# Two DRAM tables for the sums of the first mixture, and its last two tiles added by TensorE through token marks

## The reference

```python
x = x + jnp.tanh(g_xattn[0]) * _L0_xattn_ref(_layernorm(x), ctx_512, ...)
x = x + jnp.tanh(g_ffn[0]) * _L0_ffn_ref(_layernorm(x), ...)        # first mixture
x = x + jnp.tanh(g_xattn[1]) * _L1_xattn_ref(ctx_512, _layernorm(x), ...)
x = x + jnp.tanh(g_ffn[1]) * _L1_ffn_ref(_layernorm(x), ...)        # second mixture
```

## Time and profile before

| what | value |
| --- | --- |
| median of 3 runs | 369.81 us (369.34 to 369.99) |
| time of the profiled execution | 369.4 us |
| its span, first to last instruction | 367.4 us |
| TensorE busy | 322.0 us, 88% of the span |
| VectorE, ScalarE, GpSimd busy | 205.4, 153.1, 109.4 us |
| mean granted clock of TensorE | 0.896 |
| share of the chain that ended last | PE 76%, DVE 11%, ACT 4%, issue 4%, DMA 2% |

### The profile page before, as it was taken

One profiled execution on the slowest core, in us unless ns is written; L12 is line 12 of the kernel. 1 busy time (PEld: TensorE's weight loads), 2 busy tenths in 40 slices (PEclk: granted clock), 3 DMA queues, 4 the chain that ended last, 5 costly groups with the idle time before them and its releaser, 6 DMA issues.

```text
span 367.4 us, 6937 instructions
## 1 busy us (share of the span) xinstructions
PE 322.0 (88%) x2144; PEld 185.0 (50%) x2144; DVE 205.4 (56%) x640; ACT 153.1 (42%) x339; POOL 109.4 (30%) x106
## 2 busy tenths in 40 slices
PE   8974599899999999999999999158878999989992
PEld 6643493555555555555555555047334444444440
DVE  1678874655554445555555542495936645455237
ACT  1565402133444343343344444267433545445541
POOL 0021131221333332222212221133234666563310
PEclk9995556999999999999999999655869999999995
DMA  7999919996927372554211112411222222331146
GB/s 236 346 309 319 299 40 287 282 271 199 239 38 245 81 214 41 164 122 133 31 37 14 16 14 29 93 38 59 72 58 55 75 88 87 83 77 58 45 145 228
DMA packets 21146, 48.40 MB, mean 132 GB/s; under 512 B 2600, under 2 KB 11688, under 8 KB 20088
## 3 DMA queue, kind: packets, MB, share of 16 engines
q1 hardware_dynamic: 14680, 35.78, 31.0%
q0 software_dynamic: 6048, 11.28, 14.4%
q10 hardware_dynamic: 384, 0.90, 0.8%
HBM read 37.98 MB, written 9.96 MB: 131 GB/s over the span
## 4 chain that ended last, share of the span: by engine, by line
PE 76%; DVE 11%; ACT 4%; issue 4%; DMA 2%; POOL 1%; ACTq 1%; another core or an unknown queue 1%; DVEq 0%; POOLq 0%
PE bank L1432 27%; PE bank L1406 23%; PE bank L1482 8%; PE bank L1396 6%; PE bank L1245 3%; PE bank L1253 3%; PE bank L1305 2%; DVE st L749 1%; DVE z L939 1%; DMA sums<-y_sb,route_dst 1%; DVE z L827 1%; PE bank L1374 1%; DMA rows<-sums 1%; PE bank L1325 1%; POOL fs L403 1%
## 5 line engine op out<-in xcount | busy, mean ns | idle before, releaser
L1432 PE MATMUL bank<-wgu,xT 128*64 x320 | 99.5, 465 | 1.5 <-issue 0.9
L1432 PE MATMUL bank<-rows,xT 128*64 128x344 f32 x320 | 99.5, 465 | 0.0
L1406 PE MATMUL bank<-wdn,hT 120*64 (+2 forms) x396 | 89.9, 392 | 8.5 <-ACT hT L583 6.8
L1406 PEld LDWEIGHTS bank<-wdn,hT 120*64 120x64 f32 (+1 forms) x396 | 48.9, 140 | 48.4 <-issue 23.0
L1432 PEld LDWEIGHTS bank<-wgu,xT 128*64 128x64 f32 x320 | 43.1, 140 | 47.5 <-issue 8.2
L423 POOL DMA_INDIRECT sums<-y_sb,route_dst x20 | 31.6, 1581 | 115.5 <-ACT y_sb L621 97.5
L415 POOL DMA_INDIRECT x_in<-rows,route_tok x43 | 42.7, 993 | 46.3 <-DVE route_tok L945 17.6
L1019 DVE SCALAR_TENSOR_TENSOR hh<-th,bank 128x344 f32<-128x344 f32 x40 | 20.5, 513 | 58.2 <-ACT th L571 58.2
L1406 PE MATMUL bank<-rows,hT 120*64 120x256 f32 x228 | 52.4, 379 | 0.0
L1432 PEld LDWEIGHTS bank<-rows,xT 128*64 128x64 f32 x320 | 43.1, 140 | 0.0
L571 ACT ACTIVATE th<-bank 128x344 f32<-128x344 f32 x40 | 18.3, 458 | 59.3 <-PE bank L1432 59.3
(11 more groups left out here) (172 smaller groups left out, 451.6 us busy)
## 6 DMA issues: line engine op xcount, KB each, us to landing
wgu<-gu SPq DMA_DIRECT2D x8, 1376.0 KB, 22.4
wdn<-wd SPq DMA_DIRECT2D x8, 720.0 KB, 27.0
wgu<-gu SPq DMA_DIRECT2D x3, 1408.0 KB, 7.1
wdn<-wd SPq DMA_DIRECT2D x5, 576.0 KB, 8.3
rows<-rows SPq DMA_DIRECT2D x8, 256.0 KB, 3.7
wgu<-results SPq DMA_DIRECT2D x4, 512.0 KB, 5.0
wgu<-gu SPq DMA_DIRECT2D x1, 1056.0 KB, 6.8
rows<-xt SPq DMA_DIRECT2D x4, 256.0 KB, 7.4
```

The lines of the kernel that those rows point to most:

```text
L1406: last = mm(psum[7][part, 0:H], hT[0:m.wide, j * P:(j + 1) * P][:, part], wd(j), start=(j == 0), stop=(j == m.chunks - 1))
L1432: last = mm(psum[2 * c + g][part, 0:CH0], xT[:, r, k * P:(k + 1) * P][:, part], w, start=(k == 0), stop=(k == KH - 1))
```

## The change

1. `sums` has 2 * (T + P) rows. Slots 64 to 127 of a tile add to the second table: const_f has one more column, C_HALF, with T + P in rows 64 and up, and `targets` adds it to the target row. The second table is filled with zeros by one more DMA behind the five base stores, from a block of y_sb that VectorE sets to zero first. `base_stored` then counts one more.
2. Only tiles 0 to 17 are scattered (ADDED = S0 - 2). The read-back waits for 18 scatters and for all gate and up matmuls, and reads both tables: the first to xs, the second to xn, eight DMAs, from the fourth on also behind the down matmuls of tile 18.
3. Tiles 18 and 19 stay in y_sb. In steps 2 and 3 VectorE makes marks from their tokens (`mark_tokens`): for each of the 8 blocks a 128x128 matrix is_here, with a one where the slot's token is that row. Behind the last down matmuls TensorE multiplies y_sb by the marks into four PSUM banks (`first_rest` for tile 18, `add_rest` for tile 19, of which 64 slots are in use). For batches 2 and 3 TensorE also adds the rows of the second table (xn through the identity). For batches 0 and 1 VectorE adds the two tables (`two_sums`).
4. `second(b)` first adds the two PSUM blocks of the batch to xs, and then does its statistics.
5. `edge` is no longer scaled and shifted ahead of time (L1146 goes). The shift goes into nmx with one more small instruction in `mix_terms`, the scale into `add_edge`, which becomes a scalar_tensor_tensor.
6. `edges(1)` on TensorE moves behind `add_rest(0)`, and on VectorE the shifts of its half (`edge_shifts(1)`) move behind mix_terms(0). The order of `mix_terms` and `add_edge` is changed.
7. The six semaphores for the second mixture's weights become one; who waits and where stays the same.

```diff
-    sums = nc.dram_tensor("sums", (T + P, H), fp32).ap()
+    sums = nc.dram_tensor("sums", (2 * (T + P), H), fp32).ap()
...
+            sp.wait_ge(zero_made, 1)
+            sp.dma_start(sums_t[:, NT + 1:2 * NT + 2, :],
+                         y_sb[:, 0:1, :].to_broadcast([P, NT + 1, H])).then_inc(base_stored, 16)
...
-                    sp.wait_ge(y_added, 16 * S0)
+                    sp.wait_ge(y_added, 16 * ADDED)
+                    sp.wait_ge(m.gu_done, 2 * S0)
                     for b in range(B):
                         sp.dma_start(xs[:, 2 * b:2 * b + 2, :], sums_t[:, 2 * b:2 * b + 2, :]).then_inc(m.y_here[b], 16)
+                        if b == 1:
+                            sp.wait_ge(m.y_done, S0 - 1)
+                        sp.dma_start(xn[:, 2 * b:2 * b + 2, :],
+                                     sums_t[:, NT + 1 + 2 * b:NT + 3 + 2 * b, :]).then_inc(m.y_here[b], 16)
...
-                    pool.wait_ge(m.y_copied, s + 1)
-                    scatter(m, s)
+                    if m.n == 1 or s < ADDED:
+                        pool.wait_ge(m.y_copied, s + 1)
+                        scatter(m, s)
...
+            def mark_tokens(q):
+
+                tile = ADDED + q
+                then(nc.vector.scalar_tensor_tensor(
+                    out=block_of[:], in0=cf[:, C_SLOT:C_SLOT + NT], scalar=-float(P),
+                    in1=m.tok[:, tile:tile + 1].to_broadcast([P, NT]), op0=ALU.mult, op1=ALU.add))
+                nc.vector.tensor_tensor(
+                    is_here[:, q], ch[:, H_LO:H_LO + P].unsqueeze(1).to_broadcast([P, NT, P]),
+                    block_of[:].unsqueeze(2).to_broadcast([P, NT, P]), ALU.is_equal).then_inc(marked, 1)
...
+            def two_sums(b):
+
+                dve.wait_ge(mix[0].y_here[b], 32)
+                for i in (2 * b, 2 * b + 1):
+                    last = did(nc.vector.tensor_tensor(xs[:, i, :], xn[:, i, :], xs[:, i, :], ALU.add))
+                return last
+
             def second(b):
-                dve.wait_ge(mix[0].y_here[b], 16)
+
+                if b >= 2:
+                    dve.wait_ge(mix[0].y_here[b], 32)
+                dve.wait_ge(rest_done, b + 1)
+                rest = m1.late_rows[b]
+                for i in (2 * b, 2 * b + 1):
+                    last = did(nc.vector.tensor_tensor(xs[:, i, :], rest[:, i % 2, :], xs[:, i, :], ALU.add))
+                after(last)
                 stats(rows_of_x, b, LN_EPS, 1.0, x2_var)
...
-                nc.vector.scalar_tensor_tensor(out=nmx[:, two], in0=mv[:, two, 0], scalar=-1.0, in1=cc[:, two],
-                                               op0=ALU.mult, op1=ALU.mult).then_inc(mix_ready, 1)
+                then(nc.vector.tensor_tensor(nmx[:, two], mv[:, two, 0], cc[:, two], ALU.mult))
+                nc.vector.scalar_tensor_tensor(out=nmx[:, two], in0=nmx[:, two], scalar=-1.0, in1=edge_shift[:, two],
+                                               op0=ALU.mult, op1=ALU.add).then_inc(mix_ready, 1)
...
+            edge_shifts(0)
+            added = (two_sums(0), two_sums(1))
+            after(added[0])
             second(0)
+            after(added[1])
             second(1)
             mix_terms(0)
-            for b in range(B):
-                if b + 2 < B:
-                    second(b + 2)
-                if b + 1 < B:
-                    mix_terms(b + 1)
-                add_edge(b)
+            edge_shifts(1)
+            second(2)
+            add_edge(0)
+            mix_terms(1)
+            second(3)
+            add_edge(1)
+            mix_terms(2)
+            mix_terms(3)
+            add_edge(2)
+            add_edge(3)
...
+            pe.wait_ge(marked, 2)
+            pe.wait_ge(mix[0].y_copied, S0 - 1)
+            for b in range(B):
+                first_rest(2 * b)
+            add_rest(0)
+            edges(1)
+            for b in range(1, B):
+                add_rest(b)
             pe.wait_ge(edge_th, NT)
             turn_x4(0)
```

More of the change, by code:

```diff
@@ L39 @@
 ONE_LAST = most_halves(E0) < 2 * S0
+ADDED = S0 - 2
 LATE = S1 + NT - NS
@@ L187, in build @@
         w0_order, first_staged, ends_ready = sem("w0_order"), sem("first_staged"), sem("ends_ready")
-        w1_here = [sem(f"w1_here{i}") for i, _ in enumerate(second_weights())]
+        w1_here = sem("w1_here")
+        W1_ALL = 16 * sum((gu_z > gu_a) + (dn_z > dn_a) for _, gu_a, gu_z, dn_a, dn_z in second_weights())
         out_stored = sem("out_stored")
@@ L248, in __init__ @@
                             for bank in ((2, 7, 0, 1) if n == 0 else (4, 5, 3, 6))]
+                if n == 1:
+                    m.late_rows = [psum[bank][:, :].rearrange("p (j h) -> p j h", j=2) for bank in (4, 5, 3, 6)]
                 m.ranks = psum[0 if n == 0 else 2][:, 0:(NT + 1) * experts].rearrange("p (i e) -> p i e", e=experts)
@@ L694, in stage_down1 @@
                                      ACT.Copy).then_inc(m1.dn_staged, 1)
-            for n, (_, gu_a, gu_z, dn_a, dn_z) in enumerate(second_weights()):
-                act.wait_ge(w1_here[n], 16 * (gu_z > gu_a) + 16 * (dn_z > dn_a))
+            act.wait_ge(w1_here, W1_ALL)
             for i in range(NS):
@@ L960, in targets @@
                                                  ALU.is_equal, ALU.mult))
-                    nc.vector.tensor_tensor(m.dst, m.tok, m.pad, ALU.add).then_inc(m.targets_ready, 1)
+                    nc.vector.scalar_tensor_tensor(out=m.dst, in0=m.tok, scalar=cf[:, C_HALF:C_HALF + 1], in1=m.pad,
+                                                   op0=ALU.add, op1=ALU.add).then_inc(m.targets_ready, 1)
                 else:
@@ L1138, in half_var, with edge_shifts @@
                                         ALU.mult, ALU.add).then_inc(m1.var, 1)
-            dve.wait_ge(edge_c_ready, 1)
-            for h in range(2):
+            def edge_shifts(h):
                 four = slice(4 * h, 4 * h + 4)
@@ L1193, in _ @@
             dve.wait_ge(m1.experts_ready, 1)
-            for n, (_, gu_a, gu_z, dn_a, dn_z) in enumerate(second_weights()):
-                dve.wait_ge(w1_here[n], 16 * (gu_z > gu_a) + 16 * (dn_z > dn_a))
+            dve.wait_ge(w1_here, W1_ALL)
             hidden_early(2)
@@ L1498, in gate_up_slots, with add_rest, first_rest @@
                          lambda k: stage_gu1[:, t % 2, k * 2 * F1:(k + 1) * 2 * F1])
-            pe.wait_ge(mix[0].y_copied, S0)
+            def add_rest(b):
+                pe.wait_ge(mix[0].y_copied, S0)
+                rest = m1.late_rows[b]
+                if b >= 2:
+                    pe.wait_ge(mix[0].y_here[b], 32)
+                for j in range(2):
+                    i = 2 * b + j
+                    if j == 1:
+                        first_rest(i)
+                    if b >= 2:
+                        mm(rest[:, j, :], ident, xn[:, i, :], start=False, stop=False)
+                    last = mm(rest[:, j, :], is_here[0:HALF, 1, i, :], y_sb[0:HALF, (S0 - 1) % RING, :],
+                              start=False, stop=True)
+                last.then_inc(rest_done, 1)
+            def first_rest(i):
+                mm(m1.late_rows[i // 2][:, i % 2, :], is_here[:, 0, i, :], y_sb[:, (S0 - 2) % RING, :],
+                   start=True, stop=False)
+            pe.wait_ge(marked, 2)
[6 more added lines that the diff above has]
+                add_rest(b)
             pe.wait_ge(edge_th, NT)
@@ L1507, in _ @@
             ranks(m1)
-            for n, (_, gu_a, gu_z, dn_a, dn_z) in enumerate(second_weights()):
-                pe.wait_ge(w1_here[n], 16 * (gu_z > gu_a) + 16 * (dn_z > dn_a))
+            pe.wait_ge(w1_here, W1_ALL)
             for i in range(NS):
```

41 lines of the change are left out of this document (24 added, 17 removed).

## The result

| what | before | after |
| --- | --- | --- |
| median, same chip, 7 runs each | 369.99 us (369.34 to 370.72) | 372.49 us (370.99 to 373.52) |
| ratio, 95% interval | | 1.0062 (1.0045 to 1.0079) |
| profiled execution, its span | 369.4, 367.4 us | 372.8, 370.9 us |
| mean granted clock | 0.896 | 0.915 |

A forecast was written before the change was run, and what follows sets the result against it. A chain of transfers (7.9 us), then VectorE, ScalarE and TensorE bound the turn. VectorE starts 4.66 us earlier but has 5.54 us more: 0.88 us slower, median 370.7 us against 369.81; range 368.7 to 371.8.

The forecast's parts named there:

- Ahead of the turn, no cost: Before the turn, zero store, marks and loads stay hidden: zero cost, 0.2 us as the upper bound.
- I take 0.465, since it is the same engine state and place: TensorE's seven mark matmuls before the first rest_done: 0.465 us each, 3.26 us, so VectorE starts at 233.47.
- the 0.46 us for batch 1: At the turn, VectorE waits 0.46 us for batch 1's sums, from 235.34 until TensorE is through at 235.80.
- a sum of 0.88: At the turn, 5.54 us more VectorE work and waits minus 4.66 us gained: mix_terms(2) and the logits 0.88 us later.
- VectorE's other terms: At the turn: four PSUM addition pairs at 0.80 us, statistics 1.07, add_edge(1) ahead of mix_terms(2) 0.76, and small instructions.
- The rule of the Trainium skill: For VectorE's eight PSUM additions: 120 fixed cycles against SBUF's 58, 0.5 us more, median 371.2; the forecast did not adopt it.
- The rival of the held clock: From the turn through the logits, 2.4 GHz still granted at 247: logits 1.8 us shorter, median 368.9; chance 20%.
- What arrives there arrives at the end: Behind the logits (253.24), nothing changes but semaphore names, so a delay there reaches the end in full.

The follow-up runs named there:

- Run 1: The changed kernel with tile 19 multiplied by its marks over all 128 slots in place of 64; ratio to the kernel before 1.0043.
- run 2: The changed kernel with VectorE's old order, mix_terms of a batch ahead of add_edge of the batch before; ratio to the kernel before 1.0057.
- Run 7: The changed kernel with 23 filler matmuls, their results unread, in TensorE's waits from the first block's turn to the ranks; ratio to the kernel before 0.9995.
- run 9: The kernel before with filler matmuls: 48 in TensorE's wait at the turn, 10 between the logits, 6 ahead of the ranks; ratio 0.9957.
- run 4: The kernel before with only the second table added, all 20 scatters and eight additions on VectorE; ratio to the kernel before 1.0168.
- run 5: The changed kernel with 128 slots in tile 19's marks, and mix_terms of batches 2 and 3 ahead of add_edge(1); ratio to the kernel before 1.0056.
- run 6: The changed kernel with one table, TensorE adding the read-back rows of batches 1 to 3 in PSUM; ratio to the kernel before 0.9979.
- run 8: Sums in PSUM with one table, plus 18 filler matmuls in the waits of the logits and ahead of the ranks; ratio to the kernel before 0.9904.
- run 11: Sums in PSUM with fillers, plus 13 more fillers ahead of the shared expert's first two down matmuls; ratio to the kernel before 0.9876.
- run 3: The changed kernel with one table: no zero store, four read-backs, no sums of two tables; ratio to the kernel before 1.0097.

## Why the prediction was wrong

- **Ahead of the turn, no cost: right.** The first gate and up matmul is at 56.64 (56.56), the last down matmul ends at 230.11 (230.21), the zeros are all but through by 50, at 322 GB/s with the DMA engines 0.91 busy. The eight loads are issued at 223.19 to 227.66 and never waited for.
- **The failed step: "I take 0.465, since it is the same engine state and place", and with it the 0.46 us for batch 1.** State and place were the same, the shape was not: 64 and 128 rows alternate, and each change costs 0.195 us. My rows for the price were of matmuls of one height in a row: six at 0.43 and a single late weight load make the 2.79 us that I divided by six. The change has four such loads ahead of the first `rest_done`, 7 x 0.43 + 4 x 0.195 and 0.11 until VectorE starts, 3.9 us rather than 3.26. The changes cost 0.59 us at the start and 1.37 in all by batch 1. Run 1 takes them out, and 1.09 of the 2.45 us at the logits are left, against a sum of 0.88.
- **Batch 1's wait without the changes: right in size, not in its parts.** Run 1 has 0.55 us where I had 0.46. The edge scores and three marks take 2.16 us there, not 2.33, and ahead of the addition stand 0.40 us of "issue" that my sum did not have.
- **VectorE's other terms: right.** A pair out of PSUM and what follows is 0.79 from start to start (0.80), statistics 1.07, the order costs 0.80 at mix_rows by run 2 (0.76). The rule of the Trainium skill (VectorE: DVE Perf Modes, the TRN2 errata) that a PSUM source is dearer than SBUF is not borne out: the pair is busy for 0.76 us either way.
- **The rival of the held clock: its condition failed, its price was right.** The clock fell at 246.2, between two waits of TensorE for ScalarE, of 1.48 us (until 244.83) and 1.82 (until 249.01). Run 7 shows 2.1 us at the logits where I had 1.8. But the price did not end at the logits: another 0.7 us comes by the reading of the inverse, and the kernel before can have it too (run 9), so it was never a gain of this change.
- **"What arrives there arrives at the end": only on average.** Behind the logits the profiled executions differ by 1.1 us more (span - T0: 3.59 against 2.45). From the end of the logits to the reading of the inverse it takes 9.92 to 9.94 us in the kernel before and in runs 1, 2, 4, 5 and 6, where VectorE's steps end this stretch, 9.7 where the clock is held (runs 7, 8, 9 and 11), and 10.37 in the change. There the shared gate and up matmuls take 7.55 us, nearly all at 1.2 GHz, the inverse stands behind them, and TensorE leads. Of the whole the medians show little: they differ by 2.5 us.

At the logits, then, 1.36 of the 1.57 us by which the sum was short (2.45 against 0.88) are the price of the marks. That it alone carried the time out of the range is likely but not shown: run 1's ratio of 1.0043 would lie inside (371.8 is 1.0054 times 369.81), but can't be told from the change's. Between the ratios of the change on two chips, 1.0062 and 1.0098, stays a difference that I could not assign to a step, and so do part of run 5's time and of run 4's.

## What to carry to other kernels

Price a matmul by a row of the same shape and the same neighbours, and look at its weight load: filling the unused rows of a short operand can be cheaper than changing the height. Moving a start forward pays only as far as the engine that then leads has less to do; here VectorE started 4.0 us earlier and the logits came 2.45 later, so 6.5 us of new work and waits stood behind the start, and what paid was to let TensorE do the additions (run 6). And where TensorE waits ahead of a stretch that it leads, count what holding its clock would bring: 23 short fillers gave back what the change had cost.

## What the runs showed of the hardware

- A change between 64 rows and more than 64 in neighbouring fp32 matmuls of 256 columns costs 0.195 us at 2.4 GHz (0.63 against 0.43), also between 64 and 65 rows (1.05 against 0.86 for 512 columns). Between 65 and 128 rows it costs nothing (0.86, run 1), and two neighbours of 64 rows pay once (run 3). With it the weight load starts together with its matmul rather than 0.21 us ahead. The same 0.2 us stands, without a change of height, at the second mark of run 6, whose weight load had to wait for ScalarE's copy of tile 19 (0.64, start to start). Heights other than 64, 65, 120 and 128 were not run.
- How long the clock stays up behind wide matmuls is not fixed. It fell 1.4 us behind the last one in the kernel before, 3.5 in the change (last mark at 242.7, fall at 246.2), 5.2 in run 1 (238.1, 243.3), with small matmuls in between in the last two. The Trainium skill (TensorE: Matmul & The Clock Gate, the section on the HAM clock gate) has the change come on a free-running count; these distances agree.
- Once down, the clock stayed at 1.2 GHz from 248 to 262 in the change, although TensorE was busy for most of it (2.00 of 2 us in 250 to 252). With 23 short fillers, 13 of them in the two waits of 1.5 to 2 us around the point of the fall, it stayed at 2.4 GHz until 266 (run 7). What of that activity decides, the runs don't show.
